# Attention's first tiles: where the rings are cleared, and in what order GpSimd makes the first queries and the second tile's key inputs

## The reference

```
x = x + tanh(g_xattn[0]) * L0_xattn(layernorm(x), ctx)   # cross attention, 8 heads of 8 channels, rotary
x = x + tanh(g_ffn[0])   * L0_ffn(layernorm(x))          # top-2 of 8 experts and a shared one
x = x + tanh(g_xattn[1]) * L1_xattn(layernorm(x), ctx)   # gated, pooled context
x = x + tanh(g_ffn[1])   * L1_ffn(layernorm(x))          # gate, Hadamard transform, down projection
```

```
scores = einsum('bhqd,bhkd->bhqk', q, k) / sqrt(8)
out    = einsum('bhqk,bhkd->bhqd', softmax(scores), v)
```

## Time and profile before

| | us |
|---|---|
| median of 3 runs | 1402.24 (1401.1 to 1403.94) |
| profiled execution, time | 1403.49 |
| profiled execution, span | 1401.8 |

### The profile page before, as it was taken

The page is one execution under the profiler, slowest core; times in us unless marked ns, Lnnn a source line. Parts: engine busy times, 40 slices in busy tenths (PEclk is TensorE's granted clock), DMA queues, the critical chain, the costliest instruction groups (busy, mean ns, idle before and its releaser), DMA issues. The chain is left out here.

```text
span 1401.8 us, 31672 instructions
## 1 busy us (share of the span) xinstructions
PE 1324.8 (95%) x9954; PEld 1010.8 (72%) x9955; DVE 922.6 (66%) x1689; ACT 757.6 (54%) x1461; POOL 682.3 (49%) x853
## 2 busy tenths in 40 slices
PE   4899999999999789999999999999977999999998
PEld 3555555555555368888888888888876788888887
DVE  7799999999998278777554333333335676666553
ACT  0477777777777654432343333333326667666642
POOL 7677777777773148443667223310035554445210
PEclk9999999999999889999999999999976999999999
DMA  3222222222221123113743233241131111111000
GB/s 105 80 83 85 75 84 82 88 83 76 84 72 51 38 76 106 61 50 112 242 161 113 83 97 97 67 142 52 46 91 49 31 39 32 37 46 46 1 16 31
DMA packets 85890, 105.53 MB, mean 75 GB/s; under 512 B 11248, under 2 KB 76144, under 8 KB 85424
## 3 DMA queue, kind: packets, MB, share of 16 engines
q1 hardware_dynamic: 75344, 70.38, 15.8%
q0 software_dynamic: 10464, 34.09, 7.7%
HBM read 53.05 MB, written 23.99 MB: 55 GB/s over the span
## 5 line engine op out<-in xcount | busy, mean ns | idle before, releaser
L515 ACT ACTIVATE e_t<-st_ps 128x512 f32<-128x512 f32 x512 | 278.3, 597 | 103.6 <-PE st_ps L603 100.2
L432 DVE TENSOR_REDUCE row_max<-s_ps 128x4 f32<-128x1024 f32 x256 | 311.4, 1218 | 21.1 <-PE s_ps L608 19.1
L630 PE MATMUL o_ps<-e_t,v_st 128*32 128x256 f32 x2048 | 167.3, 400 | 0.0
L603 PE MATMUL st_ps<-q_st,k_st 32*128 32x256 f32 x1024 | 160.0, 333 | 5.8 <-DMA q_st<-m_rows 3.3
L608 PE MATMUL s_ps<-k_st,q_st 32*128 32x256 f32 x1024 | 157.5, 341 | 5.2 <-DVE row_max L432 3.6
L603 PEld LDWEIGHTS st_ps<-q_st,k_st 32*128 32x128 f32 x1024 | 105.8, 186 | 55.6 <-issue 40.3
L1863 POOL DMA_INDIRECT gathered_tail<-sorted_results,result_at x64 | 70.7, 1104 | 125.0 <-POOLq L2398 106.9
L1520 DVE TENSOR_TENSOR h_all_moe<-silu_moe,u_ps_moe 128x512 f32<-128x512 f32 x71 | 48.8, 687 | 107.5 <-PE u_ps_moe L1699 107.5
L1730 PE MATMUL y_ps_moe<-w_all_moe,xt_hi_moe 128*128 x568 | 112.1, 282 | 1.9 <-DVE xt_lo_moe L1514 1.9
L2129 DVE TENSOR_TENSOR h_all_tail<-silu_tail,u_ps_tail 128x512 f32<-128x512 f32 x64 | 43.8, 685 | 100.7 <-ACT silu_tail L1978 50.3
L608 PEld LDWEIGHTS s_ps<-k_st,q_st 32*128 32x128 f32 x1024 | 103.9, 192 | 7.2 <-DVE row_max L432 4.7
(11 more groups left out here) (346 smaller groups left out, 3597.4 us busy)
## 6 DMA issues: line engine op xcount, KB each, us to landing
k_st<-k_part SPq DMA_DIRECT2D x96, 128.0 KB, 2.1
q_st<-q_part SPq DMA_DIRECT2D x96, 128.0 KB
stage_first<-in_experts POOLq DMA_DIRECT2D x21, 512.0 KB
rows_in_moe<-sorted_rows SPq DMA_DIRECT2D x71, 128.0 KB, 2.1
sorted_results<-y_sb_moe SPq DMA_DIRECT2D x71, 128.0 KB, 1.7
c_in<-in_ctx SPq DMA_DIRECT2D x32, 128.0 KB, 2.2
x_sb<-in_x SPq DMA_DIRECT2D x32, 128.0 KB, 2.1
xn_moe<-in_ctx SPq DMA_DIRECT2D x8, 512.0 KB, 4.5
```

The costliest lines, as they stand in the source:

```text
L432: nc.vector.tensor_reduce(out, s_ps[p % 2][:], AX_X, ALU.max).then_inc(s["max_taken"], 1)
L515: nc.scalar.activation(e_t[t % 4][:, b, :, :], st_ps[:, b, :, :], ACT.Exp, scale=float(DH) ** -0.5)\
L603: last = nc.tensor.matmul(out, w, moving, start=True, stop=True)
L630: last = nc.tensor.matmul(o_ps[32 * j:32 * j + 32, :], values[:, at:at + 32], e_t[(2 * u + j // 2) % 4][:, j % 2, half_, :], start=(half_ ...
```

## The change

In body -2 GpSimd makes the query parts of tile 0 first and splits the context of tile 1 after that; the order was the other one. Its three clears of `q_st` 1 to 3 are gone. ScalarE makes them instead, right behind the tanh, as copies of `y_sb` (which GpSimd sets to zero at the start) broadcast over the four units. VectorE clears `k_st` 2 and 3 at p = 7 of body -2 in place of p = 7 of body -3; `k_st` 1 and `v_st` 0 stay where they were.

```diff
@@ GpSimd
-            def clear_rest():
-                for r in range(1, RING):
-                    nc.gpsimd.memset(q_st[r][:].bitcast(F32), 0.0).then_inc(s["q_cleared"], 1)
...
             def body(n, c, i):
                 if isinstance(n, int) and n == TILES:
                     first_root()
+                if isinstance(n, int) and n == -2:
+                    parts_of("q", n, c, i, 2)
                 if there(n, c, 3):
                     pool.wait_ge(c_loaded[(c + 3) % RING], 16 * uses(c, i, 3))
                     split_input("k", n + 3, c_in[(c + 3) % RING])
-                if there(n, c, 2):
+                if there(n, c, 2) and not (isinstance(n, int) and n == -2):
                     parts_of("q", n, c, i, 2)
-                if isinstance(n, int) and n == -2:
-                    clear_rest()
                 if there(n, c, 3):
                     normalize(n, 3)
@@ VectorE
                     if p == 7 and isinstance(n, int) and n == -3:
-                        clear_keys(range(1, RING))
+                        clear_keys((1,))
                         clear_values((0,))
+                    if p == 7 and isinstance(n, int) and n == -2:
+                        clear_keys((2, 3))
@@ ScalarE
             nc.scalar.activation(tanh_gain[:], gains[:], ACT.Tanh).then_inc(s["tanh_ready"], 1)
+            act.wait_ge(s["y_free"], 1)
+            for r in range(1, RING):
+                nc.scalar.copy(q_st[r][:], y_sb[:].unsqueeze(1).to_broadcast([P, UNITS, D])).then_inc(s["q_cleared"], 1)
```

## The result

| | before | changed |
|---|---|---|
| median of 21 runs each, us | 1402.34 | 1406.22 |
| ratio | | 1.0019, 95% interval [1.0011, 1.0028] |
| profiled execution: time, span | 1403.49, 1401.8 | 1406.96, 1405.2 |

The ratio times 1402.34 is +2.7 us, with an interval of 1.5 to 3.9; the forecast was +2.55. The two medians by themselves stand further apart, 3.88 us: the changed kernel's 1406.22 is 1.4 over the forecast of 1404.8 and 0.5 inside the upper end of the range. The change is small and on the slow side.

The account below looks back on a forecast made before the run. TensorE bounds steady attention; the first bodies, with GpSimd the chain, set when it fills. Sum: +2.82 + 2.14 - 0.19 - 0.84 - 1.38 = +2.55, so median 1404.8, range of 8 in 10 1402.7 to 1406.7.

Parts of the forecast that it names:

- VectorE's whole delay is carried: Rival at body 0: VectorE's chain, not m_rows, ends last, so TensorE is +3.9, 1406.2; chance 0.11.
- The steady part only carries the shift: Attention from 50 us on: TensorE is full and carries the first bodies' 2.55 to the end.
- The order on GpSimd, +2.82 to tile 1's keys: Body -2: first queries go ahead of tile 1's context split, moving its keys' rotation from 16.60 to 19.42.
- The clears return at full price, 2.14: Body -2, p = 7: VectorE's two k_st clears delay the first reduction by their full 2.14.
- GpSimd's slack takes 1.38 back: Queries of tile 1: GpSimd, formerly 1.38 late to a finished rotation, starts +2.55 late against VectorE's +3.93.
- The first plain scores: TensorE, tile 0: scores move from about 20.2 to about 22.7, behind tile 1's key projection.
- The hand-over by `m_rows`: SyncE's queue to TensorE: m_rows issued at 42.5, transposed scores at 44.59, +2.55, again behind that transfer.
- ScalarE's copies cost nothing: Behind the tanh: three q_st copies take 3.1 within ScalarE's 10.96 idle before the values' copy; cost 0.
- swallowed: Rival in bodies 1 to 4: slack in ScalarE or VectorE absorbs up to all the delay, 1402.2; chance 0.06.
- The clock's own term: TensorE's rise from its slower level: a slow microsecond loses 0.28; the rise moving otherwise has chance 0.12.
- the rival of a rise that stays where it is: Clock rival: the rise keeps its time while work moves 2.55, 0.7 comes back, 1404.1; clock otherwise 0.12.
- GpSimd's relief: Rival at tile 1's query projection: the removed 2.73 of clears makes it 0.8 earlier, 1401.4; chance 0.05.

Follow-up runs that it names:

- e5: The changed kernel with GpSimd's old order in body -2; transposed scores shifted -0.36 us, ratio 1.0008 against the kernel before.
- e4: The changed kernel with k_st 2 and 3 cleared on ScalarE instead of VectorE; transposed scores shifted +0.35 us, ratio 1.0017 against the kernel before.
- e2: The kernel before with only VectorE's clears of k_st 2 and 3 moved to body -2; transposed scores shifted +0.10 us, ratio 1.0021.
- e6: The changed kernel with VectorE's clears of k_st 2 and 3 back in body -3; shift +1.21 us, ratio 1.0012 against the kernel before.
- e1: The kernel before with only GpSimd's new order, its three clears kept behind the context split; shift +1.20 us, ratio 1.0019.
- e8: The kernel before with only the q_st clears moved from GpSimd to ScalarE, run a second time; shift -2.22 us, ratio 0.9990.
- e3: The kernel before with only the three q_st clears moved from GpSimd to ScalarE; shift -2.25 us, ratio 0.9993.
- e10: The kernel before with ScalarE's q_st clears, m_rows first in SyncE's queue in body 0, and extra unread TensorE products; ratio 1.0020.

## Why the prediction was right

- *The number.* The ratio gives +2.7 for a forecast of +2.55. The median of 1406.22 lies 1.4 over the forecast and is, taken by itself, the number of the rival in which VectorE's whole delay is carried (1406.2). It is the trace that tells the two apart: the shift is +2.43, and what stands on top of it comes after attention or is spread between runs.
- *The steady part only carries the shift.* Shown: +2.44 at the copy of 49.32, +2.35 at that of 445.57.
- *The order on GpSimd, +2.82 to tile 1's keys.* Measured 19.43 - 16.60 = 2.83; worth 2.79 at the changed kernel's transposed scores (e5).
- *The clears return at full price, 2.14.* Measured 2.08 by e4. e2 shows that this holds only because the swap has made VectorE the later chain: alone the move costs 0.1.
- *GpSimd's slack takes 1.38 back, and its removed clears are worth nothing here.* Shown by the 5.10 wait and by e6 = e1.
- *The first plain scores.* By the prediction's own terms they are at 20.2 + 2.82 = 23.0, not 22.7, and they came at 22.44: before, TensorE had waited 0.51 for the transfer of `q_part` at 20.19, and this wait is gone. It cost nothing, since VectorE comes to them only at 25.75.
- *The hand-over by `m_rows`.* Issued at 42.39 (42.5 forecast), scores at 44.49 (44.59), still held by that transfer.
- *ScalarE's copies cost nothing.* Three took 2.92, from 7.86 (3.1 forecast), and ScalarE was then idle for 10.65 before the values' copy at 21.43.
- *The rivals.* VectorE's whole delay was not carried: its last reduction of body 0 is at 49.63 against 47.19, +2.44, as late as TensorE and no more. Nothing was swallowed. The clock's own term was mis-sized: a slow microsecond cost 0.33 over long stretches and 0.1 in the pair at hand, not 0.28, and the rise lies anywhere between 48 us (e8) and 66 us (e4), not 3 us around the work. In a single execution it can be larger than the effect; that it averages out over 21 runs is not shown. In the pair at hand the rise moved 1.0 us while the work moved 2.44, which is in part the rival of a rise that stays where it is. e3 and e8 have the turn 7.36 us apart. The Trainium skill's TensorE: Matmul & The Clock Gate, section "What's actually happening", says that the turn moves from run to run, but by 500 ns either way; these two differ by far more. In e10 TensorE was booked as busy 5.00 of 5.00 for 20 us at a granted clock of 0.50. The same section of the Trainium skill says that activity releases the slow state; the busy time in these rows does not bear that out.
- *One price was wrong.* The prediction gave GpSimd's relief 0.8, by the one wait it saw on TensorE at 23.92. The first paragraph of the same text had GpSimd as the chain all the way to `m_rows`, and GpSimd came 1.38 late to a finished rotation; by that the relief is worth up to the 2.73 of the clears, until VectorE ends last, and e3 measured 2.25. It did not touch the forecast, since the rival was ruled out by the order, but it hid that one of the three edits, taken alone, starts the transposed scores earlier.

## What to carry to other kernels

Where two engines run side by side into a hand-over, an edit's worth is the move of the later chain, so three edits of -2.25, +0.10 and +1.20 can make +2.43: price them together, and then try each alone, since one may be a gain that the others bury. Before a step is moved earlier on one engine, read the list of the engine that uses it: here TensorE had another product ahead, and what had been pushed back to make room was what it waited for. Here VectorE's two clears, ahead of its wait for TensorE, moved only its next rotation (13.79 for 12.64, and GpSimd came to it later still); behind that wait they cost 2.08.

## What the runs showed of the hardware

- In the first 47 us of all the kernels without extra products TensorE runs at the lower level (128 x 256 products of 0.41 us) although the rows' granted clock is 1.00; in e10, where the level had changed once by then, the same product lasts 0.41 and the clock reads 0.50, and 0.27 with the clock at 1.00. So in these traces the 1.00 ahead of a kernel's first change of level tells nothing, and the duration of a known product does.
- The level's rise differed by 7 us between two executions of one kernel (e3 and e8, on two chips) and was worth 2.4 us, as much as the whole change.
- A copy of a broadcast 128 x 256 source to 128 x 1024 fp32r on ScalarE took 2.92 / 3 = 0.97 us, near VectorE's clear of the same size (0.91).
